# Three single-pass products in place of f32 matmuls in the values and in the last feed-forward's second layer

## The reference

```python
x = x + 0.5 * ffn(layernorm(x))
x = x + attn(layernorm(x))      # causal, 16 heads of 16
x = x + 0.5 * ffn(layernorm(x))
# ffn: h = x @ W_exp + b_exp, butterfly(up), gelu(h + up_bias), butterfly(down), @ W_con + b_con + down_bias
# attn: softmax(QK'/4 with causal mask) V, then the output projection WO
```

## Time and profile before

| | us |
|---|---|
| median of three runs | 2054.3 |
| lowest, highest | 2054.05, 2055.82 |
| the profiled execution's own time | 2052.31 |
| its span (first to last instruction) | 2050.6 |
| TensorE busy | 1981.8 (97%) |
| VectorE busy | 1683.8 (82%) |
| ScalarE busy | 1336.8 (65%) |
| GpSimd busy | 257.6 (13%) |

### The profile page before, as it was taken

One profiled execution on the slowest core, in us unless ns is written; L12 is line 12 of the kernel. 1 busy time (PEld: TensorE's weight loads), 2 busy tenths in 40 slices (PEclk: granted clock), 3 DMA queues, 4 the chain that ended last, 5 costly groups with the idle time before them and its releaser, 6 DMA issues.

```text
span 2050.6 us, 58320 instructions
## 1 busy us (share of the span) xinstructions
PE 1981.8 (97%) x23992; PEld 1209.2 (59%) x23992; DVE 1683.8 (82%) x3658; ACT 1336.8 (65%) x1583; POOL 257.6 (13%) x723
## 2 busy tenths in 40 slices
PE   2799999999999999999999999999999999999999
PEld 1677777655555555555555555555555555578887
DVE  7744566599999999999999999999999999536562
ACT  3432222388888888888888888888888888753321
POOL 7400000010101111011110101111011110110000
PEclk9999999999999999999999999999999999999999
DMA  7012111221111111111111121111211110101110
GB/s 205 26 72 76 49 49 55 91 56 43 41 52 41 45 42 44 47 42 49 45 44 41 40 53 40 46 42 45 47 41 50 44 42 26 50 24 62 62 42 21
DMA packets 93241, 104.20 MB, mean 51 GB/s; under 512 B 25552, under 2 KB 55856, under 8 KB 92720
## 3 DMA queue, kind: packets, MB, share of 16 engines
q1 hardware_dynamic: 92272, 100.23, 17.4%
q0 software_dynamic: 704, 0.25, 0.2%
HBM read 70.54 MB, written 29.36 MB: 49 GB/s over the span
## 4 chain that ended last, share of the span: by engine, by line
PE 92%; DVE 3%; SPq 2%; ACT 1%; DMA 1%; issue 0%; DVEq 0%; ACTq 0%
PE PS L1144 32%; PE PS L1262 31%; PE PS L1121 12%; PE PS L1094 6%; PE PS L1242 6%; PE PS L1193 1%; PE PS L1115 1%; PE PS L1060 1%; SPq L379 1%; DVE OA L813 1%; SPq L383 0%; DVE OA L918 0%; ACT PG L633 0%; ACT OA L614 0%; DVE MXP L942 0%
## 5 line engine op out<-in xcount | busy, mean ns | idle before, releaser
L709 ACT ACTIVATE PG<-PS 128x1024 f32<-128x1024 f32 (+1 forms) x1152 | 1117.5, 977 | 238.4 <-PE PS L1242 175.8
L942 DVE TENSOR_REDUCE MXP<-PS 128x1 f32<-128x512 f32 x1792 | 1099.2, 684 | 18.1 <-PE PS L1144 18.0
L1242 PE MATMUL PS<-QT,KT 50*128 50x512 f32 (+1 forms) x2304 | 810.7, 431 | 0.0
L1144 PE MATMUL PS<-KT,QT 48*128 48x512 f32 (+3 forms) x2304 | 795.9, 431 | 2.6 <-DVE MXP L942 2.3
L1262 PE MATMUL PS<-PG,VH 128*17 128x128 f32 x16896 | 725.9, 276 | 0.1
L1262 PEld LDWEIGHTS PS<-PG,VH 128*17 128x17 f32 x16896 | 400.1, 96 | 415.5 <-issue 367.2
L1144 PEld LDWEIGHTS PS<-KT,QT 48*128 48x128 f32 x2304 | 340.0, 184 | 251.6 <-issue 143.4
L1242 PEld LDWEIGHTS PS<-QT,KT 50*128 50x128 f32 x2304 | 339.3, 184 | 10.3 <-issue 10.1
L938 DVE CUSTOM_DVE_ANT_0 PS<-PS,MASK 128x128 f32<-128x128 f32 (+3 forms) x512 | 249.1, 506 | 72.7 <-PE PS L1144 66.3
L571 POOL TENSOR_SCALAR_AFFINE_SELECT PG<-PG 128x128 f32<-128x128 f32 x512 | 136.4, 292 | 999.2 <-ACT PG L709 998.4
L1121 PE MATMUL PS<-MD,PG 128*128 128x256 f32 x1024 | 233.4, 382 | 1.6 <-ACT PG L633 1.6
(11 more groups left out here) (114 smaller groups left out, 898.4 us busy)
## 6 DMA issues: line engine op xcount, KB each, us to landing
QT<-q_parts SPq DMA_DIRECT2D x256, 64.0 KB
KT<-k_parts SPq DMA_DIRECT2D x256, 64.0 KB
q_parts<-OA SPq DMA_DIRECT2D x16, 512.0 KB, 2.8
QT<-q_parts SPq DMA_DIRECT2D x256, 32.0 KB
k_parts<-OA SPq DMA_DIRECT2D x16, 512.0 KB, 4.7
KT<-k_parts SPq DMA_DIRECT2D x256, 32.0 KB
o_parts<-OS SPq DMA_DIRECT2D x128, 64.0 KB
OA<-o_parts SPq DMA_DIRECT2D x32, 256.0 KB
```

What stands on the lines that cost most here:

```text
L709: nc.scalar.activation(PB[n % 2][half][:, :, q0:TILE], PS[:, half * 1024:half * 1024 + 1024].rearrange("p (k q) -> p k q", k=2)[:, :, q0:T ...
L942: nc.vector.tensor_reduce(dst, bank(b), AX.X, ALU.max).then_inc(mx_red, 1)
L1144: mm(bank(4 + qs % 2 if b is None else b, w), q[0:SC, (BT * place(j) + qs) * P:(BT * place(j) + qs + 1) * P].bitcast(f32r), k[0:SC, c * TI ...
L1242: last = mm(PS[:, (2 * half + k) * 512 + q0:(2 * half + k + 1) * 512], CK[0:SM, kb * P:(kb + 1) * P].bitcast(f32r), CQ[0:SM, place(j) * TI ...
```

## The change

- The values: WV gets a rounded part and a remainder like WQ and WK (third entries of WH and WL), and each value block is three single-pass products of X2H and X2L with them. XT2A and `whole_rows` go; xt_rdy is now raised by VectorE's X2L. WV is loaded into the tail of V, and the setting of V's column of ones waits for w_low.
- The second layer of the second pass (not that of the first phase): ScalarE makes each Gelu twice, rounded into GH (over KT) and whole into G; GpSimd makes the remainder GL (over QT) after each bias addition (`low_hidden`); VectorE splits MD into MDH and MDL (over WH, WL, X2H, X2L) after the first normalisation of the second pass, before it takes the first transposed rows; TensorE makes three products per block of 128 hidden units (`y2_blocks`), of which the first row block waits for each GL part. A tile's Gelus wait, from the second tile on, until the GL of the tile before is complete.
- To make room, OS0 to OS2 are one tile OS3, and OB2 lies in it.

```diff
@@ -109,18 +109,21 @@
         MD = sb("MD", [P, HB, D])
-        WQ, WK, WV, WO = (sb(n, [P, DK, D]) for n in ("WQ", "WK", "WV", "WO"))
+        WQ, WK, WO = (sb(n, [P, DK, D]) for n in ("WQ", "WK", "WO"))
         XN = sb("XN", [P, BT, D])
-        XTH, XTL, X2H = (sb(n, [P, DK, TILE]) for n in ("XTH", "XTL", "X2H"))
-        X2L = sb("X2L", [P, DK, TILE])
-        WH, WL = sb("WH", [P, 2, DK, D]), sb("WL", [P, 2, DK, D])
+        XTH, XTL = (sb(n, [P, DK, TILE]) for n in ("XTH", "XTL"))
+        X2 = sb("X2", [P, PARTS, DK, TILE])
+        X2H, X2L = X2[:, 0, :, :], X2[:, 1, :, :]
+        W2 = sb("W2", [P, PARTS, 3, DK, D])
+        WH, WL = W2[:, 0, :, :, :], W2[:, 1, :, :, :]
         G = PG
...
-        XN2A, XT2A = (OA[:, 4 * i:4 * i + 4, :] for i in range(2))
-        OS = [sb(f"OS{i}", [P, P]) for i in range(O_BUFFERS)]
+        XN2A = OA[:, 0:BT, :]
+        OS3 = sb("OS3", [P, O_BUFFERS, P])
+        OS = [OS3[:, i, :] for i in range(O_BUFFERS)]
         MASK = sb("MASK", [P, TILE + 3 * P], bf16)
@@ -133,7 +136,7 @@
         OB = sb("OB", [P, D])
-        OB2 = sb("OB2", [P, D])[:, :]
+        OB2 = OS3[:, 0:D // P, :].rearrange("p a b -> p (a b)")
         BNS = sb("BNS", [P, NB, 6])
@@ -169,7 +172,10 @@
-        XT2A = XT2A.rearrange("p a b -> p (a b)").rearrange("p (k t) -> p k t", k=DK)
+        GH, GL = (t[:, :].rearrange("p (b t) -> p b t", b=HB) for t in (KT, QT))
+        MDH = W2[:, :, :, :, :].rearrange("p a w k d -> p (a w k d)")[:, 0:HB * D].rearrange("p (b d) -> p b d", b=HB)
+        MDL = X2[:, :, :, :].rearrange("p a k t -> p (a k t)").rearrange("p (b d) -> p b d", b=HB)
         CK, CQ, NK, NQ = KT[0:NEXT, :], QT[0:NEXT, :], KT[NEXT:P, :], QT[NEXT:P, :]
@@ -186,6 +192,8 @@
         FU, FD = fold_scratch(oa), fold_scratch(vv)
+        V_TAIL = W_LEN + 4 * HID
+        WV = vv[:, V_TAIL:V_TAIL + DK * D].rearrange("p (k d) -> p k d", k=DK)
         BW = D + 1
@@ -232,6 +240,7 @@
         os_ev, out_done = sem("os_ev"), sem("out_done")
+        mdh_rdy, mdl_rdy, gl_rdy = sem("mdh_rdy"), sem("mdl_rdy"), sem("gl_rdy")
@@ -584,8 +593,16 @@
+            def low_hidden(k):
+                for b in range(HB):
+                    pool.wait_ge(gelu_done, (k + NT) * HB + b + 1 + FREE_H)
+                    nc.gpsimd.tensor_tensor(GL[:, b, :].bitcast(f32r), G[:, b, :], GH[:, b, :], ALU.subtract
+                                            ).then_inc(gl_rdy, 1)
             for k in range(NT):
                 add_bias(tile_at(k), k + 2 * NT)
+                low_hidden(k)
@@ -630,6 +647,8 @@
                     src = bank(turn_bank("h", n * HB + b) if isinstance(n, int) and n < NT else 2 + b % 4)
+                    if n >= NT:
+                        nc.scalar.activation(GH[:, b, :].bitcast(f32r), src, ACT.Gelu, bias=GB[:, b:b + 1])
                     nc.scalar.activation(G[:, b, :], src, ACT.Gelu, bias=GB[:, b:b + 1]
@@ -645,14 +664,9 @@
-            def whole_rows(t):
-                act.wait_ge(x2_rdy, t + 1 + (t == NT - 1))
-                nc.scalar.activation(XT2A, PS[:, 0:DK * 512].rearrange("p (k t) -> p k t", k=DK), ACT.Copy
-                                     ).then_inc(xt_rdy, 1)
             def high_weights():
                 act.wait_ge(in_proj, 64)
-                for i, w in enumerate((WQ, WK)):
+                for i, w in enumerate((WQ, WK, WV)):
                     nc.scalar.activation(WH[:, i, :, :].bitcast(f32r), w[:, :, :], ACT.Copy
@@ -686,7 +700,6 @@
                 if t:
-                    whole_rows(t - 1)
                     high_parts(t - 1)
@@ -725,8 +738,11 @@
             for k in range(NT - 1):
+                if k:
+                    act.wait_ge(gl_rdy, k * HB)
                 gelus(k + NT, y_f2(k) - 1)
                 std(k + NT + 3, slice(0, BT))
+            act.wait_ge(gl_rdy, (NT - 1) * HB)
             gelus(2 * NT - 1, Y_LAST)
@@ -850,7 +866,7 @@
                 nc.vector.tensor_tensor(X2L[:, :, :].bitcast(f32r), src, X2H[:, :, :], ALU.subtract
-                                        ).then_inc(x2_rdy, 1)
+                                        ).then_inc(xt_rdy, 1)
@@ -990,6 +1006,7 @@
                             dve.wait_ge(at_ps, 2)
+                            dve.wait_ge(w_low, 3)
                             nc.vector.memset(V[:, :, :, DH:DV], 1.0)
@@ -1022,6 +1039,9 @@
             normalize(XN, tile_at(0), None)
+            nc.vector.tensor_copy(MDH.bitcast(f32r), MD[:, :, :]).then_inc(mdh_rdy, 1)
+            dve.wait_ge(mdh_rdy, 1)
+            nc.vector.tensor_tensor(MDL.bitcast(f32r), MD[:, :, :], MDH, ALU.subtract).then_inc(mdl_rdy, 1)
             take_transposed_parts(NT, seq_f2(0))
@@ -1111,9 +1131,12 @@
                         pe.wait_ge(v_ev, t * BT + b + 1)
+                    cols = slice(b * P, (b + 1) * P)
                     for k in range(DK):
-                        last = mm(y_bank(b), XT2A[:, k, b * P:(b + 1) * P], WV[:, k, :],
-                                  start=(k == 0), stop=(k == DK - 1))
+                        high, low = WH[:, 2, k, :], WL[:, 2, k, :]
+                        for i, (x, wt) in enumerate(((X2H, high), (X2H, low), (X2L, high))):
+                            last = mm(y_bank(b), x[:, k, cols].bitcast(f32r), wt.bitcast(f32r),
+                                      start=(k == 0 and i == 0), stop=(k == DK - 1 and i == 2))
                     last.then_inc(v_ps, 1)
@@ -1178,16 +1201,19 @@
                     if t == 1:
-                        pe.wait_ge(w_low, 2)
+                        pe.wait_ge(w_low, 3)
                         pe.wait_ge(in_proj, 64)
-                    pe.wait_ge(x2_rdy, t)
+                    if t < NT:
+                        pe.wait_ge(xt_rdy, seq_p(t - 1) + 1)
+                    else:
+                        pe.wait_ge(x2_rdy, 1)
                     for w in range(4):
...
                             if t == NT and w == 0 and k:
-                                pe.wait_ge(x2_rdy, t + 1)
+                                pe.wait_ge(xt_rdy, seq_p(t - 1) + 1)
                             high, low = WH[:, w // 2, k, cols], WL[:, w // 2, k, cols]
@@ -1310,6 +1336,18 @@
+            def y2_blocks(k, y, blocks):
+                for b in blocks:
+                    pe.wait_ge(y_ev, y * BT + b + 1)
+                    cols = slice(b * P, (b + 1) * P)
+                    for i in range(HB):
+                        if b == 0:
+                            pe.wait_ge(gl_rdy, k * HB + i + 1)
+                        for w, g in ((MDH, GH), (MDL, GH), (MDH, GL)):
+                            last = mm(y_bank(b, y), g[:, i, cols].bitcast(f32r), w[:, i, :].bitcast(f32r),
+                                      start=(i == 0 and w is MDH and g is GH), stop=(i == HB - 1 and g is GL))
+                    last.then_inc(y_ps, 1)
             def up2(k):
@@ -1322,13 +1360,13 @@
                 y_blocks(y_w(k + 1), range(BT), XT2B, WO, DK)
-                pe.wait_ge(gelu_done, (k + NT) * HB + HB + FREE_H)
-                y_blocks(y_f2(k), range(BT - 1), G, MD, HB)
+                if k == 0:
+                    pe.wait_ge(mdl_rdy, 1)
+                y2_blocks(k, y_f2(k), range(BT - 1))
                 transposes(XN, xn_rdy, k + 2 * NT + 1, seq_f2(k + 1))
-                y_blocks(y_f2(k), range(BT - 1, BT), G, MD, HB)
+                y2_blocks(k, y_f2(k), range(BT - 1, BT))
             up2(NT - 1)
-            pe.wait_ge(gelu_done, 2 * NT * HB + FREE_H)
-            y_blocks(Y_LAST, range(BT), G, MD, HB)
+            y2_blocks(NT - 1, Y_LAST, range(BT))
```

## The result

The changed kernel takes 2032.17 us (median of 6 runs, 2029.55 to 2038.79), the kernel before 2055.29 us beside it (6 runs, 2054.05 to 2057.54): ratio 0.989, 95% interval 0.9874 to 0.9905. That is 23.1 us less by the medians; the interval of the ratio, times 2055, spans 19.5 to 25.9. The profiled execution took 2032.39 us, its span is 2030.7 us, so it lies 19.9 us under the profiled execution of before, and, unlike that one, at its own kernel's median.

The account below looks back on a forecast made before the run. TensorE was taken to carry the chain without a gap in the second pass; 20.2 us from the second layer plus 4.8 from the values, 25.0 off 2052.3, gave 2027.3, plus 2.0 for the median, stated as 2029.5 us; range 2022 to 2037.

Parts of the forecast that it names:

- The 2.0 us that the forecast added: Whole kernel: the median of the runs before lay 2.0 us above the profiled execution, so 2027.3 became 2029.3, stated as 2029.5.
- Price of a product: TensorE: a single-pass 256-column product costs 0.116 us, three 0.348 against 0.432 for one f32 matmul; bounds 0.109 to 0.190.
- the 0.3 set aside for the split: Second pass, VectorE's split for the next up products: 0.05 us a tile for semaphore and weight load, 0.3 in all.
- Rivals 2 and 3: Second layer, values: 2, weight load unhidden, 2098 or 2130 us, chance 0.05; 3, products at 0.109 us, 2023 us, chance 0.09.
- rival 5: Whole kernel: the change does not act, the products being issued as before; 2054 us, chance 0.02.
- rival 1: Second pass: GpSimd's low parts cost 1.51 us, perhaps held off by VectorE's multiply, late each tile; 6 us, 2035.5, chance 0.13.
- The 0.4 us at block 2: Second layer: block 2 needs the bank freed by block 0's residual at 1923.9 and starts at 1924.4, 0.4 us to spare.
- the tight split: Next tile's up products: VectorE's split ends at 1932.55, TensorE gets there at 1932.8; named as what is late next.
- the 0.25 us around an evacuation: First phase, values: ends and semaphores around the 0.38 us evacuation put at 0.25, so a bank returns after 0.63 us.
- the 0.2 for the copy: First phase: ScalarE's whole-row copy, 8 x 1.02 us, goes; given 0.2 us saved in all.
- the 0.04 us lost twice a tile at a bank's return: First phase, values: bank back at 0.63 us, next load wants it at 0.59; 0.6 us lost in all.
- Rival 4: First phase: the values bring nothing because VectorE's maxima give the pace; 4.8 us less saved, 2034.5 us, chance 0.1.

Follow-up runs that it names:

- remainder_twice: Changed kernel with each of GpSimd's subtractions issued twice, one behind the other: 2121.77 us, ratio 1.0308.
- two_products: Changed kernel without the product of MD's low part with the hidden layer's high part in the second pass's second layer: 2021.9 us, ratio 0.9813.
- half_columns: Changed kernel with 128 instead of 256 moving columns in the second layer's products, half the output features left out: 2031.17 us, ratio 0.9861.
- values_only: Changed kernel with the second layer as before, so only the first phase's values in three products: 2051.54 us, ratio 0.9984 to the kernel before.

## Why the prediction was right, and where it was off

The forecast was 25.0 us off the profiled execution; the profiled one of after has 19.9. The 5.1 us between are: 0.7 in the second layer, 2.75 in the values (4.8 forecast, 2.05 seen, about 1 of the difference being the clock's shorter fall in before's profile), 1.7 in the start-up, which no run tells from scatter. The 2.0 us that the forecast added for "the median lies above the profile" were not needed for after, and made up for part of it: 2029.5 against 2032.2. That part of the agreement is luck. The mechanism stood: TensorE carries the chain, three products cost less than one f32 matmul, and the splitting is hidden beside them in every tile but the last.

- **Price of a product.** 0.116 forecast, 0.119 measured, well inside 0.109 to 0.190; the term missed by 0.003 us a product, 0.28 a tile (2.69 forecast, 16.9 / 7 = 2.41 measured), 1.9 in seven tiles, and the 0.3 set aside for the split was not spent. Seven tiles: 18.8 - 0.3 forecast, 16.9 measured. The load is hidden: products follow every 0.119 us while a load of theirs is recorded at 0.189 (0.190 in the earlier trace rows). Rivals 2 and 3 fall with this number, and rival 5 with the time. After, the loads' row:

```profile
L1347 PEld LDWEIGHTS PS<-X,KT 128*128 128x128 f32 x256 | 48.3, 189 | 0.0
```

  The Trainium skill, page "TensorE: Matmul & The Clock Gate", section "Part 3: Packing small matmuls — row/col tiling", lists that a load overlaps a matmul only when the row groups differ; the trace disagrees here as it did before. The same section also lets a load into the background weight buffer go ahead of running matmuls, which the trace doesn't contradict: read so, the section gives no loss.
- **ScalarE.** Taken was 2 x 0.69 = 1.39 us a pair from the earlier trace rows, whose three Gelus take 2.08 us together. That row merges three with a wait of 0.13 us before the third. By time, before and then after:

```profile
1907.18 0.69 ACT L633 ACTIVATE PG<-PS,GB 128x512 f32<-128x512 f32 x1
1907.77 0.68 ACT L633 ACTIVATE PG<-PS,GB 128x512 f32<-128x512 f32 x1
```

```profile
1979.38 0.69 ACT L651 ACTIVATE KT<-PS,GB 128x512 fp32r<-128x512 f32 x1
1979.96 0.68 ACT L652 ACTIVATE PG<-PS,GB 128x512 f32<-128x512 f32 x1
```

  Recorded at 0.69, they start 0.57 to 0.59 apart, in before already: 1.14 a pair in after. The prediction mistook records that overlap for a pace. It made no error in the steady tiles, where the pairs are hidden, but it is why the last tile saved 2.6 us and not 1.7: the last low part is ready 14.3 us after the up products start (2007.34 + 10.03 - 2003.06), not 15.2. What sets the pace of the last tile is GpSimd (L600 x7 in the chain, 1.25 each), not the pairs.
- **GpSimd.** 1.25 each where nothing collides (10.03 / 8), as forecast, and 1.37 in the tiles with VectorE's multiply; the eighth is ready at 1980.72 + 10.96 = 1991.68 and wanted at 1990.96 + 7 x 0.357 = 1993.46, 1.8 us to spare (1.6 forecast). The lock of rival 1 acts:

```profile
1980.72 10.96 POOL L600 TENSOR_TENSOR QT<-PG,KT 128x512 fp32r<-128x512 f32 x8 [9.16 <-ACT PG L652]
...
2007.34 10.03 POOL L600 TENSOR_TENSOR QT<-PG,KT 128x512 fp32r<-128x512 f32 x8 [9.14 <-ACT PG L652]
```

```profile
1983.54 2.06 DVE L1030 TENSOR_TENSOR OA<-OA 128x1024 f32<-128x1024 f32 x1
```

  VectorE's multiply takes 2.06 us beside the subtractions, 1.23 before, and the eight take 0.93 us more than in the last tile, which has no multiply (in `remainder_twice` it is one subtraction that takes 2.16 us for 1.26). The Trainium skill, page "SBUF — State Buffer", section "SBUF: two separate sides", states such an exclusive lock; the trace agrees in that each of the two engines has an operation prolonged. It costs nothing here: the 1.8 us to spare are what is left with it, and TensorE waits for no VectorE operation in these tiles. Rival 1's mechanism was there and its 1.51 us were not.
- **VectorE.** The 0.4 us at block 2 and the tight split were the right places, and `two_products` and `half_columns` show that these are next. At block 2 the number came out (0.5 to 0.6 measured) without its reason: the prediction took the residual's time over from before (1923.50) and didn't say why a shorter block 0 wouldn't move it. It is because the residual stands behind the whole normalisation of the next tile, which starts from WO's last residual.
- **Split of MD.** 3.5 us instead of 4.9, done long before the transposes at 1796.8:

```profile
1786.91 1.22 DVE L1042 CAST W<-MD 128x2048 fp32r<-128x2048 f32 x1
1788.16 2.29 DVE L1044 TENSOR_TENSOR X<-MD,W 128x2048 fp32r<-128x2048 f32 x1
```

- **Values.** The term that was mis-sized: 4.8 forecast, 2.05 in this pair, 2.7 to 4.0 with the clock alike. A tile's products save 0.58 us, not 0.68. Of it 0.09 goes where TensorE goes over to f32, and more in the tiles where it now waits for the keys' transfer, which the prediction didn't look at. The six tiles between the transposes at 102.9 and 349.8 us of before take 246.9 us, and 244.8 in after: 2.1 us saved instead of 4.1 (246.84 to 246.95 in the four profiles with f32 values, 243.88 to 245.14 in the ten without: 1.7 to 3.1). No run shows the 0.25 us around an evacuation or the 0.2 for the copy that goes by themselves. Of the 0.04 us lost twice a tile at a bank's return, the tile at 236 us shows about as much once: its products start 0.12 us apart, but 0.145 at the third block and 0.129 at the fourth. Rival 4, that they bring nothing, falls by `values_only`, whose interval excludes it.

## What to carry to other kernels

Single-pass products in threes pay where TensorE has no gap and the splitting fits beside it; take the price of an operation from the spacing of starts in a stream, not from its recorded length: on TensorE and on ScalarE the records overlap. When a stage gets shorter, redo the sum for what is hidden beside it, following each engine's queue in its order: dropping a third of these products brought 11 of their 30 us, because VectorE's normalisation stood ahead of the residual that frees a bank. Where work behind a shortened piece needs a transfer, ask how much sooner it can come before the transfer is late, and count on part of the gain only. And compare two profiles by stage only where the granted clock is alike in both: here one short stretch near 390 us hid 1 us of the values' gain.

## What was not expected of the hardware

- An idle engine costs twice: after waits of 1.3 to 2.3 us each TensorE was granted 1.2 GHz for a while, in `remainder_twice` 2.0 us on top of each tile's wait. Near 390 us the same fall lasts 3.4 us in one profile and 6.8 in the ten others without fillers, and it came back soon after for 10 us in one and for 34 in another. Seven unread products of 256 columns in the idle time kept the clock up there in all three profiles that have them.
- TensorE loses 0.075 us where it goes over from single-pass to f32 products: the first of these is followed after 0.29 us instead of 0.216 (at 239.56 us in after; 0.08 or 0.09 a tile in all ten profiles with split values).
- A 128x2048 cast on VectorE takes 1.22 us, a subtraction of the same size 2.29.
- Half the columns hardly make a product cheaper: 0.112 us with 128, 0.119 with 256. Twice as many cost 0.228.
